# One result before the second scatter, and the second image's attention taken two steps at a time

## The reference

```python
x = layer0(x)   # group norm, qkv, softmax attention of 4 heads of 32 channels, projection, + x
t = tokens(x)
t = t + layer1_attn(ln(t))  # K softmaxed over tokens, Q over channels of a head; out = Wr (K V^T) Q
t = t + layer1_ffn(ln(t))   # router: top 2 of 8 experts; per expert LN affine, W1, gelu, W2
x = from_tokens(t)
```

## Time and profile before

| | |
|---|---|
| time, median of 3 runs (lowest, highest) | 361.16 us (359.86, 362.2) |
| the profiled execution: its time, its span | 362.47 us, 360.7 us |
| PE, DVE, ACT, POOL busy | 315.8, 198.4, 195.0, 113.5 us |
| chain that ended last, by engine | PE 71%, DVE 13%, POOL 5%, issue 4%, ACT 3%, DMA 2% |
| its largest lines | PE L919 17%, L896 9%, L1160 8%, L1138 8%; POOL L530 4% |
| mean granted TensorE clock | 0.915 of 2.4 GHz |

### The profile page before, as it was taken

One profiled execution on the slowest core, in us unless ns is written; L12 is line 12 of the kernel. 1 busy time (PEld: TensorE's weight loads), 2 busy tenths in 40 slices (PEclk: granted clock), 3 DMA queues, 4 the chain that ended last, 5 costly groups with the idle time before them and its releaser, 6 DMA issues.

```text
span 360.7 us, 6258 instructions
## 1 busy us (share of the span) xinstructions
PE 315.8 (88%) x1885; PEld 196.0 (54%) x1885; DVE 198.4 (55%) x620; ACT 195.0 (54%) x305; POOL 113.5 (31%) x192
## 2 busy tenths in 40 slices
PE   7979899999999989999999798946580499999986
PEld 3533434344444434445432436746580399999985
DVE  1586435575757654564568537478540057776510
ACT  1370657677677745555576204672350187787722
POOL 2074193000000001000304771051277836556530
PEclk9996969999999999999999859996596599999999
DMA  6059886753000034000000113000011322224215
GB/s 196 4 120 207 185 188 269 191 180 122 0 2 3 3 106 129 0 2 1 2 0 24 45 37 74 8 9 8 9 52 59 103 61 69 75 72 120 92 42 222
DMA packets 20540, 27.88 MB, mean 77 GB/s; under 512 B 3831, under 2 KB 14508, under 8 KB 20252
## 3 DMA queue, kind: packets, MB, share of 16 engines
q1 hardware_dynamic: 15800, 17.57, 18.2%
q0 software_dynamic: 3520, 9.39, 8.3%
q10 hardware_dynamic: 1188, 0.53, 0.6%
HBM read 11.15 MB, written 8.33 MB: 54 GB/s over the span
## 4 chain that ended last, share of the span: by engine, by line
PE 71%; DVE 13%; POOL 5%; issue 4%; ACT 3%; DMA 2%; DVEq 1%; SPq 0%; POOLq 0%; ACTq 0%
PE ps L919 17%; PE ps L896 9%; PE ps L1160 8%; PE ps L1138 8%; PE ps L877 5%; PE ps L861 4%; POOL expert_in L530 4%; PE ps L756 2%; PE ps L955 2%; PE ps L828 2%; PE ps L796 2%; DVE pm L1275 1%; PE ps L946 1%; DMA Qs<-mrow 1%; PE ps L1117 1%
## 5 line engine op out<-in xcount | busy, mean ns | idle before, releaser
L598 ACT ACTIVATE probs<-ps 128x1024 f32<-128x1024 f32 x64 | 65.3, 1020 | 33.0 <-PE ps L896 32.9
L919 PE MATMUL ps<-probs,vT 128*32 128x512 f32 x256 | 69.4, 618 | 0.6 <-ACT probs L598 0.5
L919 PE MATMUL ps<-probs,ones 128*32 128x512 f32 x256 | 69.4, 618 | 0.0
L466 POOL TENSOR_TENSOR rstd<-ve,minus_half 128x8 f32<-128x8 f32 (+1 forms) x8 | 11.0, 1384 | 143.9 <-DVE ve L1326 76.4
L1272 DVE CUSTOM_DVE_ANT_0 above<-ps,above 128x512 f32<-128x512 f32 x56 | 38.7, 691 | 31.6 <-PE ps L877 29.8
L1138 PE MATMUL ps<-w,GT 128*128 x312 | 44.8, 290 | 9.0 <-ACT GT L734 9.0
L536 POOL DMA_INDIRECT token_out<-Y,yidx x39 | 37.7, 966 | 45.3 <-DVE Y L1606 43.0
L1618 DVE TENSOR_TENSOR H<-ps,b1T 128x512 f32<-128x512 f32 x39 | 27.0, 692 | 35.8 <-PE ps L1160 33.2
L1138 PEld LDWEIGHTS ps<-w,GT 128*128 128x128 f32 x312 | 40.6, 203 | 10.4 <-issue 10.3
L1160 PE MATMUL ps<-XTT,w1s 128*128 128x128 f32 x312 | 45.4, 293 | 0.2 <-ACT XTT L712 0.2
L896 PE MATMUL ps<-Qs,Ks 98*128 98x512 f32 x128 | 44.1, 426 | 1.2 <-issue 0.7
(11 more groups left out here) (233 smaller groups left out, 437.5 us busy)
## 6 DMA issues: line engine op xcount, KB each, us to landing
XR<-expert_in SPq DMA_DIRECT2D x39, 65.0 KB
Qs<-q_hi SPq DMA_DIRECT2D x16, 128.0 KB, 3.1
w<-in_L_ffn_W SPq DMA_DIRECT2D x1, 2048.0 KB, 8.4
w<-in_L_ffn_W SPq DMA_DIRECT2D x8, 256.0 KB, 4.3
YG<-token_out SPq DMA_DIRECT2D x8, 256.0 KB, 3.8
Ks<-k_hi SPq DMA_DIRECT2D x14, 128.0 KB, 2.4
expert_in<-zeros POOLq DMA_DIRECT2D x1, 1300.0 KB, 5.7
expert_in<-zeros POOLq DMA_DIRECT2D x1, 1235.0 KB, 8.1
```

Source lines behind the costliest of these rows:

```text
L598: nc.scalar.activation(probs[:, s % 3, :], bank(2 + 2 * (s % 2), 2), ACT.Exp).then_inc(exp_done, 1)
L919: last = nc.tensor.matmul(bank(value_bank(o))[i * HD:(i + 1) * HD, :], w, probs[:, s % 3, hd * HALF:(hd + 1) * HALF], start=kt == 0, stop= ...
```

## The change

`SENT_FIRST` goes from 4 to 1. `rsqrt(B + 2)` moves from behind ten of `scatter(0)`'s DMAs to behind six. The loop over steps 32 to 63 goes by twos on PE. The parts of layer 1 are laid on later steps, PE's on even ones, so that `counts` moves from step 56 to step 60 and `project` from 34 to 36. For the second image `queryT`, `context`, `fold` and `attend` (on DVE `attend stats`, on ACT `queryT_sb`) go ahead of the expert steps, and `tokenT` goes behind step 0.

```diff
-    SENT_FIRST = 4
+    SENT_FIRST = 1
...
-        LAYER1_AT = {BEGIN_LAYER1: "centre residual", 34: "project", 35: "tokens_stats tokens", 38: "keys",
-                     40: "keys_exp", 41: "query_value0", 42: "query_value1", 43: "keyT query_max",
-                     44: "keyT_sb queries_exp", 45: "queries context", 46: "queries_scaled fold", 47: "queryT",
-                     48: "queryT_sb", 49: "attend stats", 50: "tokenT", 51: "tokenT_sb", 52: "logits shift",
-                     53: "gates_exp", 54: "route choose norm2_0", 55: "norm2_1", 56: "norm2_2 counts", 57: "norm2_3"}
-        LAYER1_PE = {"before": "residual project query_value0 query_value1 keys values keyT", "first": "queryT context",
-                     0: "fold attend", "1 mid": "tokenT", 1: "logits", 2: "counts"}
-        LAYER1_DVE = {"before": "tokens_stats tokens query_value0 query_value1 keys queries queries_scaled context fold",
-                      0: "attend stats", 1: "logits shift route choose", 2: "counts"}
-        LAYER1_ACT = {"before": "tokens_stats", "staged": "queries_exp keys_exp values keyT_sb", "0 mid": "queryT_sb",
-                      "1 mid": "tokenT_sb", 1: "gates_exp norm2_0 norm2_1 norm2_2 norm2_3"}
+        LAYER1_AT = {2 * STEPS + 2: "centre", 36: "residual project", 37: "tokens_stats tokens", 40: "keys",
+                     41: "keys_exp", 42: "query_value0", 44: "query_value1", 46: "keyT query_max",
+                     47: "keyT_sb queries_exp", 48: "queries context", 49: "queries_scaled", 50: "fold queryT",
+                     51: "queryT_sb", 52: "attend stats", 54: "tokenT", 55: "tokenT_sb", 56: "logits shift",
+                     57: "gates_exp", 58: "route choose norm2_0", 59: "norm2_1", 60: "norm2_2 counts", 61: "norm2_3"}
+        LAYER1_PE = {"before": "residual project query_value0 query_value1 keys values keyT queryT context fold attend",
+                     0: "tokenT", 1: "logits", 2: "counts"}
+        LAYER1_DVE = {"before": "tokens_stats tokens query_value0 query_value1 keys queries queries_scaled context fold "
+                                "attend stats",
+                      1: "logits shift route choose", 2: "counts"}
+        LAYER1_ACT = {"before": "tokens_stats", "staged": "queries_exp keys_exp values keyT_sb queryT_sb",
+                      "0 mid": "tokenT_sb", 1: "gates_exp norm2_0 norm2_1 norm2_2 norm2_3"}
...
-            scatter(0, lambda j: rsqrt(B + 2) if j == J - 3 else None)
+            scatter(0, lambda j: rsqrt(B + 2) if j == J - 5 else None)
...
+            for s in range(2 * STEPS, UNITS * STEPS, 2):
+                both_scores(s + 1)
+                both_scores(s + 2)
+                if s == 2 * STEPS + 2:
+                    pe.wait_ge(consts_ready, 2)
+                    pe.wait_ge(ld_rows, 16 * 4)
+                run_parts(layer1, LAYER1_AT, s, 0)
+                both_values(s)
+                run_parts(layer1, LAYER1_AT, s + 1, 0)
+                both_values(s + 1)
...
                     x_transpose(1)
-                    run_parts(layer1, LAYER1_PE, "first", 1)
```

More of the change, by code:

```diff
@@ L1084, in _, with both_scores, both_values @@
                 scores(0, 0, hd)
-            for s in range(UNITS * STEPS):
+            def both_scores(s):
+                if s < UNITS * STEPS:
+                    for hd in range(2):
+                        scores(s // STEPS, s % STEPS, hd)
+            def both_values(s):
+                for hd in range(2):
+                    values(s // STEPS, s % STEPS, hd)
+            for s in range(2 * STEPS):
                 new = new_slots(s)
@@ L1088, in _ @@
                     max_first(g)
-                if s + 1 < UNITS * STEPS:
-                    for hd in range(2):
-                        scores((s + 1) // STEPS, (s + 1) % STEPS, hd)
+                both_scores(s + 1)
                 for g in new[0:1]:
```

## The result

The changed kernel took 359.15 us (median of 20 runs, 357.05 to 360.9) against 361.7 (median of 20, 19 of them 359.84 to 363.83). The ratio is 0.9935, 95% interval 0.9913 to 0.9957: a gain of 2.35 us, within the 1% that the prediction called no change, where it said 5.4 us and 355.8.

The account below looks back on a forecast made before the run. The start of scatter(1) was taken to bound the last quarter. With the addresses at 255.8 instead of 249.83, its first DMA goes at 256.0 instead of 261.44: 361.16 - 5.4 = 355.8 us, range 351.8 to 361.6.

Parts of the forecast that it names:

- a rival of 0.16: Second image's attention: the clock falls, 3.0 us per spell ahead of logits, giving 361.8, with three spells 364.8; chance 0.16.
- The gain of the first scatter line: scatter(1)'s first DMA behind send(1) to send(3) on POOL: SENT_FIRST = 1 gives 11.6 us with the addresses unmoved.
- What was to hide the late results: Results 1 to 8, sent behind scatter(1), go in a queue nobody reads before the end; 16 buffers hold them.
- Pairs: PE's steps 32 to 63 by twos: 0.30 us saved per pair, 4.8 for 16, 3.6 for the 12 ahead of logits.
- the waits: Second image's attention on PE: new waits of 1.3 at step 44, 0.8 at step 50, 1.8 at queryT; together 3.9 us.
- DVE late at `norm(7)`: First image's v_slots on DVE ends at 203.8, norm(7) only then: +3.5 us for the second image's layer 1.
- attend to logits: Second image, with tile 0's work and the gelu in between: 8.9 us instead of 4.84, +4.1 (bounds 1 and 6).
- 1.9 us of slack: Tile 0's rows come at 233.5, ahead of attend's end at 235.4; beyond 1.9 us they would push tokenT.
- logits to addresses: Second image: logits to mask takes 7.2 us instead of 8.36, -1.2; the addresses stay 6.36 behind mask.
- pairs save nothing: Rival: pairs bring no saving on PE, logits comes 3.6 us later and all behind it, 359.4; chance 0.14.
- DVE in time: Rival: waits of 3.9 mostly absorbed, norm(7) waits for PE as before, the 3.5 are not paid, 352.3; chance 0.14.
- a drain at the gelu's table: Rival: the gelu's table switch in the second image brings a drain of 1.4 us, 357.2; chance 0.04.

Follow-up runs that it names:

- sent1_alone: The kernel before with SENT_FIRST = 1 and nothing else: 350.47 us, ratio 0.9708 to the kernel before.
- experiment 4: Also spelled sent1_pairs: the kernel before with SENT_FIRST = 1 and PE's loop over steps 32 to 63 by twos, old table of parts: 350.45 us, 0.9707.
- after_norm5_late: The changed kernel with norm(5) on DVE at step 51 instead of 49, behind fold: 356.63 us, 0.9869 to the kernel before.
- after_sent4: The changed kernel with SENT_FIRST = 4 again: 369.39 us, 1.0223 to the kernel before.
- experiments 6 to 9: Kernel before with SENT_FIRST = 1 and new order behind the attention (0.9728); changed kernel with first table part behind norm(7) (0.9823), norm(5) at step 51 (0.9869), both (0.9809).
- experiment 9: The changed kernel with the first image's v_slots table part behind norm(7) and norm(5) at step 51: 355.02 us, 0.9809 to the kernel before.
- experiments 3: The changed kernel with PE's loop over steps 32 to 63 one step at a time, new tables kept: 357.2 us, 0.9899 to the kernel before.
- experiment 7: The changed kernel with the first image's v_slots table part moved behind norm(7) on DVE: 355.73 us, 0.9823 to the kernel before.
- sent1_table1_late: The kernel before with SENT_FIRST = 1 and the second image's table part behind expert step 6: 349.79 us, 0.9676 to the kernel before.
- sent1_tail_first_table1_late: The kernel before with SENT_FIRST = 1, second image's table part behind expert step 6, its layer 1 up to choose ahead of the expert steps: 352.45 us, 0.9754.

## Why the prediction was wrong

The direction and the mechanism were right, the sum was not: 5.4 us were forecast and 2.35 came. The step that failed is the clock inside the second image's attention. The sum put it at nothing and left it to a rival of 0.16; it fell behind `queryT` and cost 1.6 us, so that `logits`, and with it `project`, came 1.4 us later than forecast. The rest is 0.9 us for the second scatter's slow first DMAs, which had no term, 0.6 from `attend` to the addresses (3.5 for 2.9) and 0.2 ahead of `attend`. From the common start, beside sent1_alone:

- **The gain of the first scatter line**, 11.6 us with the addresses where they were: 10.5 measured. What was to hide the late results held, but the scatter itself was slower by 0.9 us, since its first DMAs now run beside `v_slots`' table part. Before, this part was long done when the scatter began. This term was missing.
- **Pairs**: 0.30 us each was right as an issue time (0.33), and the waits were nearly right (1.26, 0.46, 1.87 for 1.3, 0.8, 1.8). The 0.33 fits the rule of the Trainium skill, "TensorEngine Tiling (Array Packing)", section "Key Properties", that a change of tiling mode drains the engine. But what pairs save on PE reaches `logits` only as far as no exp and no product of DVE is due, and no part stands between a pair's two values (experiment 4).
- **The clock.** The sum kept it at full in the attention and left the fall to a rival at 3.0 us a spell. One spell came, behind `queryT`: 1.6 us (14.08 - 13.44 = 0.64, plus the 1.0 that three pairs should have saved). In after_norm5_late, where the wait is 0.61 and the clock stays up, the same stretch took 12.44, 1.64 less. The prediction had named a clock below 1.00 there as a sign of being wrong. `logits` was forecast 6.65 us later than before and came 8.03 later. The forecast of what follows from `logits` to `project`, 206.7 - 185.9 = 20.8, was met: 20.82. So 4.9 instead of 3.5 were lost at `project`.
- **DVE late at `norm(7)`** was right in place and size: with the table part moved, PE's wait is 3.2 us shorter and the kernel 4.0 faster.
- **attend to logits**: 4.6 more than sent1_alone's for a forecast of 4.1. Tile 0's two transposes waited 0.49 and 0.25 us, where 1.9 us of slack was counted; the profile puts the second down to the rows' DMA, the first to issue. POOL's wait for the variance in `scatter(0)` was 3.66 us (1.20 before, and about 1 more was counted). Five other kernels with the new order (after_sent4 and experiments 6 to 9) have neither wait, and `logits` 8.74 or 8.75 behind `attend`. But their addresses come 22.98 to 23.24 behind `attend`, no earlier than the 22.61 here, so no profile shows that the late rows cost the addresses anything. The gelu's table cost what its row says, no drain.
- **logits to addresses**: 1.1 less, forecast 1.2. In those five kernels it is 14.2 to 14.5, against sent1_alone's 14.30, so the forecast was met here by luck.

Together 4.9 - 0.2 + 4.6 - 1.1 = 8.2 us lost instead of 6.0, and 0.9 at the scatter: 11.5 - 8.2 - 0.9 = 2.4, as measured. That it closes so well is luck too: one stage of one profile varies by 1.5 us and more (experiment 9). Of the rivals, "pairs save nothing" (359.4) has the right time, and experiments 3 and 4 bear it out for the end result, though not in its reason. "DVE in time" is out by experiment 7, a drain at the gelu's table by its row. The later start of layer 1 is the costliest part of the change: 8.6 us by itself, of which the place of `rsqrt(B + 2)` makes 2.0 in its profile by the wait alone; on the old table pairs ran too, at the same time as single steps. What stays open is small: whether single steps on the new table are faster than pairs (1.3 us by the ratio, 0.7 at `project` in the two profiles), what the new order behind the attention costs by itself, and why the clock fell in sent1_pairs.

## What to carry to other kernels

When an in-order queue holds the critical transfer behind waits of no urgency, move that transfer first and measure this alone: every other edit in the same change is then judged by what it does to the time at which the transfer's input is ready. A saving on one engine counts only up to the next wait for another engine; walk from wait to wait, not from sum to sum. And ask of each wait you add whether PE's clock falls behind it, for the price of the fall can be as large as that of the wait.

## What the runs showed of the hardware

An indirect DMA on POOL took 0.96 us. It took 1.64 or 1.56 where it started 0.11 to 0.18 us into a 128 x 720 comparison on DVE, 1.18 to 1.20 some 0.05 into a 128 x 240 product, and 1.62 to 1.90 (one DMA of `scatter(0)` in each of six kernels) 0.16 to 0.45 into a 128 x 1024 product. In all 26 cases over the runs it ended 0.82 to 0.85 us behind the end of the DVE operation. What it lost is therefore what was left of that operation, less some 0.13 us: one that started 0.28 into a product of 0.41 us (sent1_table1_late) took 0.96, and so did one that started 0.24 ahead of the comparison. One case does not fit: started 0.04 into a product it took 0.96, and the product 0.48 instead of 0.41 (sent1_tail_first_table1_late). All these DVE operations read two tiles of SBUF; over 400 DMAs that started during one with an input from PSUM (`ps`) took 0.95 to 0.98.

The clock fell after 1.87 us of idle in pairs and stayed up after 1.54 in single steps. In sent1_pairs it fell with no wait ahead of it, 0.4 us behind the end of `logits`' sixteen matmuls of 8 columns; in sent1_alone it stayed up behind the same matmuls. Behind the 1.89 us ahead of `project` it stayed low for 13.7 or 6.8 us in two profiles of the same code. The prediction took one profile's spell for the price of that stage; as it stood on both sides of the difference, it cancelled.
